# Third aggregation of a graph network: transposed sums, layer products in pairs, later routing, a ring of 14 groups

## What is computed

```python
x = x + gin(layernorm(x), edges)            # two sums over neighbours, four layers
x = x + slice_attention(layernorm(x))
# here the change begins: the sum over neighbours of a GCN layer
h = layernorm(x) @ W
out = segment_sum(h[src] * dinv[src] * dinv[dst], dst) + b
x = x + relu((out - mean) * rsqrt(var + 1e-5) * gamma + beta)
# top-2 of 8 experts, 256 -> 512 -> 256, weights by a softmax of the two gate values
x = x + moe(layernorm(x))
```

## Time and profile before

| what | value |
|---|---|
| median of three timed runs | 4080.15 us |
| the profiled execution, its span | 4526.2 us (the page has no time beside its span) |
| PE, POOL busy | 75%, 62% of the span |
| third aggregation | 2783 to 4060 us: 1277 us |
| its gathers | 846, from 2783.0 to 4009.8 us |
| expert stage | 4060 to 4526 us |

### The profile page before, as it was taken

The page is one execution under the profiler, slowest core; times in us unless marked ns, Lnnn a source line. Parts: engine busy times, 40 slices in busy tenths (PEclk is TensorE's granted clock), DMA queues, the critical chain, the costliest instruction groups (busy, mean ns, idle before and its releaser), DMA issues. The chain is left out here.

```text
span 4526.2 us, 40559 instructions
## 1 busy us (share of the span) xinstructions
PE 3407.3 (75%) x12357; PEld 2256.3 (50%) x12359; DVE 1481.5 (33%) x5707; ACT 497.8 (11%) x1161; POOL 2794.2 (62%) x2815
## 2 busy tenths in 40 slices
PE   3577777878878889899999976566556656658997
PEld 2354444545453444444444455345444444438986
DVE  5112121212121433444333445234343343442221
ACT  4010000000110000000000002000000000003432
POOL 4666666666646666666666502666666666635664
PEclk7788888988889999999999987777777778769998
DMA  6333333433349666666666527334334333327887
GB/s 199 90 112 112 111 110 110 131 111 111 109 128 330 194 198 200 193 190 194 195 201 205 170 104 240 108 114 123 115 117 128 115 114 114 119 80 174 203 210 188
DMA packets 321341, 687.10 MB, mean 152 GB/s; under 512 B 58976, under 2 KB 148300, under 8 KB 320854
## 3 DMA queue, kind: packets, MB, share of 16 engines
q0 software_dynamic: 169712, 474.01, 37.9%
q10 hardware_dynamic: 86448, 110.35, 7.4%
q1 hardware_dynamic: 64970, 100.14, 6.8%
HBM read 592.43 MB, written 99.13 MB: 153 GB/s over the span
## 5 line engine op out<-in xcount | busy, mean ns | idle before, releaser
L280 POOL DMA_INDIRECT s_edge_rows<-table,w_src_idx x2538 | 2495.4, 983 | 1235.3 <-issue 712.6
L320 PE MATMUL s_psA<-s_edge_rows,s_onehot 128*128 128x257 f32 (+2 forms) x4932 | 1695.0, 487 | 212.1 <-DMA s_edge_rows<-table,w_src_idx 92.3
L320 PEld LDWEIGHTS s_psA<-s_edge_rows,s_onehot 128*128 128x128 f32 x4932 | 1012.6, 210 | 758.6 <-issue 635.1
L295 DVE TENSOR_SCALAR s_onehot<-w_iota_row,w_dst_l 128x128 f32<-128x128 bf16 x2466 | 531.6, 296 | 28.5 <-PEq L149 16.4
L2031 POOL DMA_INDIRECT acc_rows<-s_y,s_tnode x105 | 166.3, 1584 | 130.7 <-DVE s_y L2154 98.8
L1011 PE MATMUL s_psM<-s_h1T,s_w1b 128*128 128x512 f32 (+2 forms) x448 | 195.2, 582 | 52.5 <-ACT s_h1T L913 49.0
L330 PE MATMUL s_psA<-s_edge_rows,s_early 128*128 128x257 f32 (+2 forms) x648 | 221.3, 468 | 10.2 <-issue 9.0
L1017 PE MATMUL s_psM<-s_w2a,s_hT 128*128 128x512 f32 x392 | 196.3, 647 | 22.7 <-issue 16.6
L2179 PE MATMUL s_psU<-s_xT,s_w 128*128 128x128 f32 x1680 | 208.2, 278 | 0.2 <-ACT s_xT L2085 0.2
L2179 PEld LDWEIGHTS s_psU<-s_xT,s_w 128*128 128x128 f32 x1680 | 199.3, 195 | 0.6 <-issue 0.6
L2189 PE MATMUL s_psD<-moe_w,s_hT 128*128 x840 | 199.5, 381 | 0.0
(11 more groups left out here) (364 smaller groups left out, 2802.6 us busy)
## 6 DMA issues: line engine op xcount, KB each, us to landing
s_w<-in_L_ffn_W_dram SPq DMA_DIRECT2D x105, 512.0 KB
s_edge_rows<-table,w_src_idx POOLq DMA_INDIRECT x2538
s_swT<-swt_rows SPq DMA_DIRECT2D x12, 1024.0 KB
table<-s_trow ACTq DMA_DIRECT2D x11, 1024.0 KB
own_rows<-s_own ACTq DMA_DIRECT2D x11, 1024.0 KB
s_self_h<-own_rows ACTq DMA_DIRECT2D x11, 1024.0 KB
swt_rows<-s_swT ACTq DMA_DIRECT2D x11, 1024.0 KB
extra_rows<-w_zeros SPq DMA_DIRECT2D x7, 896.0 KB
```

The costliest lines, as they stand in the source:

```text
L280: pool.indirect_dma_start(self.rows[:, g % self.SLOTS, t, :], None, self.table, bass.IndirectOffsetOnAxis(ap=src_idx[:, at:at + 1], axis=0 ...
L295: last = nc.vector.tensor_scalar(into[:, t, :], iota_row[:, q * P:(q + 1) * P], dst_l[:, at + t:at + t + 1], None, ALU.is_equal)
L320: last = nc.tensor.matmul(banks[b % 2][:, 0:w], self.onehot[:, g % self.AHEAD, t, :], self.rows[:, g % self.SLOTS, t, col:col + w], start= ...
```

## The change

It touches the third aggregation alone (`pipeline` gets an argument that the others leave at 0).

- The rows are the weights now and the one-hots the moving operand (`turned_sums`), once for each half of the 256 features. So `psA` holds the sums transposed, and ScalarE copies them straight into `aggT` (`close`). `agg`, the addition on VectorE and the transposes go.
- The own rows are added by PE: two products of `self_v` with the identity matrix, ahead of a block's last group. `self_v` and `extra` have two buffers and are loaded one super-block ahead.
- The ring of gathered groups has 14 slots instead of 6.
- Layer products, scalings and the transposes of `TURNED` go in pairs of blocks, through two whole banks. The scaling (`SCALED`) is a piece of its own, one step behind the product, and so are `TOP` behind `GATES` and `COUNTED` behind `RANK`. The gate products go to `psR`.
- `USED` is at 22 to 25: these four steps run within the next super-block's pieces (`late`), and `at_lane` and `at_tile` have eight buffers instead of four.

```diff
-        def pipeline(group, close, piece, begin=None, close_first=False):
+        def pipeline(group, close, piece, begin=None, close_first=False, late=0):
+            def pieces(s, k):
+                if 0 <= s < len(SUPER):
+                    piece(s, k)
+                if 0 <= s - 1 < len(SUPER) and k < late:
+                    piece(s - 1, STEPS + k)
...
+            def turned_sums(self, pe, b, i, banks, s_free):
...
+                for t in range(n):
+                    for k in range(self.turned):
+                        last = nc.tensor.matmul(banks[b % 2][:, k * P:(k + 1) * P], self.rows[:, g % self.SLOTS, t, k * P:(k + 1) * P],
+                                                self.onehot[:, g % self.AHEAD, t, :],
...
-            PRODUCT, NORM, TURNED, GATES = (0, 1, 2, 3), 4, (7, 8, 9, 10), 11
-            CHOICE, RANK, PLACED, USED = 12, 16, (17, 18, 19, 20), (18, 19, 20, 21)
-            edges = Edges(S, table3, D, ((0, D),), FP32, 1, slots=6)
+            PRODUCT, SCALED, NORM, TURNED, GATES = (1, 3), (2, 4), 5, (9, 10), 12
+            TOP, CHOICE, RANK, COUNTED = 13, 14, 16, 18
+            PLACED, USED = (19, 20, 21, 22), (22, 23, 24, 25)
+            LATE_STEPS = USED[-1] + 1 - STEPS
+            edges = Edges(S, table3, D, ((0, D),), FP32, 1, slots=14, turned=KD)
...
                 def close(b):
                     s, q = place_of(b)
-                    act.wait_ge(s_tr, b + 1)
-                    ac.activation(aggT[:, :, q * P:(q + 1) * P], psT[0][:, 0:D].rearrange("p (k n) -> p k n", k=KD),
-                                  ACT.Copy).then_inc(s_aggT, 1)
+                    if q == 0 and s:
+                        act.wait_ge(s_o, pairs(s)[0][0])
+                    act.wait_ge(edges.s_used, groups_before(b + 1))
+                    ac.activation(aggT[:, :, q * P:(q + 1) * P], psA[b % 2][:, 0:D].rearrange("p (k n) -> p k n", k=KD),
+                                  ACT.Copy).then_inc(s_evac, 1)
...
-                    dve.wait_ge(edges.s_used, groups_before(b + 1))
-                    dve.wait_ge(s_both_self, s + 1)
-                    v.tensor_tensor(agg[:, q, :], self_v[:, q, :], psA[b % 2][:, 0:D], ALU.add).then_inc(s_evac, 1)
...
-                    edges.sums(pe, b, g, psA, s_evac)
+                    if g == groups_of(b) - 1:
+                        s, q = place_of(b)
+                        pe.wait_ge(s_both_self, s + 1)
+                        for k in range(KD):
+                            last = mm(psA[b % 2][:, k * P:(k + 1) * P], self_v[:, s % 2, q, k * P:(k + 1) * P], ident[:, :],
+                                      start=False, stop=False, skip_group_check=True)
+                        last.then_inc(s_own, 1)
+                    edges.turned_sums(pe, b, g, psA, s_evac)
...
-                    pe.wait_ge(s_evac, b + 3)
-                    pe.wait_ge(s_aggT, b + 1)
-                    for k in range(KD):
-                        last = nc.tensor.transpose(psT[0][:, k * P:(k + 1) * P], agg[:, q, k * P:(k + 1) * P], ident[:, :])
-                    last.then_inc(s_tr, 1)
```

More of the change, by code:

```diff
@@ L200, in pipeline @@
                         if s and i == 2 + k * (len(turns) - 2) // STEPS:
-                            piece(s - 1, k)
+                            pieces(s - 1, k)
             close(NB - 1)
             for k in range(STEPS):
-                piece(len(SUPER) - 1, k)
+                pieces(len(SUPER) - 1, k)
+            for k in range(late):
+                pieces(len(SUPER), k)
         def place_of(b):
@@ L1654, in build @@
             s_dve = S.sem("dve_chain")
-            s_self = S.sem("self_rows")
+            s_self = [S.sem(f"self_rows{i}") for i in range(2)]
             s_both_self = S.sem("self_rows_summed")
@@ L1678, in build, with pairs @@
             block = stack.enter_context(nc.Block())
+            def pairs(s):
+                first = sum((nb + 1) // 2 for _, nb in SUPER[:s])
+                return [(first + p, 2 * p, min(2, SUPER[s][1] - 2 * p)) for p in range((SUPER[s][1] + 1) // 2)]
             @block.gpsimd
@@ L1817, in piece @@
                     b0, nb = SUPER[s]
[L1818 to L1819 removed]
+                    if k in SCALED[0:len(pairs(s))]:
+                        at, j, n = pairs(s)[SCALED.index(k)]
                         if j == 0:
@@ L1916, in piece @@
                             pe.wait_ge(s_we, 16)
-                            pe.wait_ge(s_aggT, b0 + nb + 1)
-                        pe.wait_ge(s_acc, b0 + j + 1)
-                        for c in range(KD):
-                            last = mm(psO[(b0 + j) % 2][:, 0:D], aggT[:, c, j * P:(j + 1) * P], w[:, c, :], start=c == 0, stop=c == KD - 1)
-                        last.then_inc(s_o, 1)
-                    if k in TURNED[0:nb]:
-                        j = TURNED.index(k)
-                        if j == 0:
-                            pe.wait_ge(s_gread, s + 1)
-                        pe.wait_ge(s_xl, b0 + j + 5)
-                        pe.wait_ge(s_t1c, b0 + j + 1)
-                        for c in range(KD):
-                            last = nc.tensor.transpose(psT[1][:, c * P:(c + 1) * P], xl3[:, j, c * P:(c + 1) * P], ident[:, :])
+                        pe.wait_ge(s_evac, b0 + j + n + 2)
@@ new lines, in piece @@
+                        pe.wait_ge(s_acc, at + 1)
+                        for i in range(j, j + n):
+                            for c in range(KD):
+                                last = mm(psO[at % 2][:, (i - j) * D:(i - j + 1) * D], aggT[:, c, i * P:(i + 1) * P], w[:, c, :],
+                                          start=c == 0, stop=c == KD - 1)
+                        last.then_inc(s_o, 1)
+                    if k in TURNED[0:len(pairs(s))]:
+                        at, j, n = pairs(s)[TURNED.index(k)]
+                        pe.wait_ge(s_xl, b0 + j + n + 4)
+                        pe.wait_ge(s_t1c, at + 1)
+                        for i in range(n):
+                            for c in range(KD):
+                                last = nc.tensor.transpose(psT[at % 2][:, (2 * c + i) * P:(2 * c + i + 1) * P], xl3[:, j + i, c * P:(c + 1) * P], ident[:, :])
```

117 lines of the change are left out of this document (67 added, 50 removed).

## The result

| kernel | median | range | runs |
|---|---|---|---|
| before | 4080.15 us | 4075.96 to 4080.58 | 5 |
| changed | 4092.51 us | 4090.22 to 4096.16 | 5 |

The ratio is 1.0029, 95% interval 1.0018 to 1.0040: the changed kernel is 12 us slower. The forecast was 4047 us, 33 us faster.

What follows compares the result with a forecast made beforehand. GpSimd's gathers, one per 1.26 us, were taken to pace the third aggregation, with 149.8 us of stops. From 4080.15, 30 (a fifth of the stops) and 3.4 (tail) were subtracted, giving 4047 us, range 3918 to 4100.

Steps and rivals of the forecast that it cites:

- The bound: Third aggregation: GpSimd's 846 gathers, one per 1.26 us, are the pacer, at least 1066 us in the profiled execution.
- The 150 us of stops: Third aggregation: GpSimd stands still 149.8 us beyond its gather rhythm, where the ring of six groups is full.
- the loop PE, VectorE, PE: Third aggregation: ring stops are paid through PE and VectorE waiting in turn; such waits end at L1907, 180.7 us idle.
- From the profile to the clock: Whole kernel: 446 us of the 4526.2 us profile do not exist when timed; 30 of 149.8 us taken as gained.
- the two readings: Where the 446 us lie: first, stops in three aggregations, 449.5 us; second, gathers of 1.00 us when timed, 440 us.
- Own rows: Third aggregation: 98 PE products, 22 us, replace 98 transposes and 49 VectorE additions; the wait at L1907 goes.
- no work is added: Third aggregation, pairs and later routing: same products and copies, fewer handovers, no added work.
- Transposed sums: Third aggregation: shorter, more numerous PE instructions add 16 us of PE work; cost on the path 0, bounds -0 and +16.
- Head and tail: Third aggregation: a 3.3 us head stop, part of the 149.8; at the end 3.96 us shrink to 0.5, saving 3.4.
- No stops when timed: Third aggregation: gathers pace it throughout, so deeper ring and shorter loop give nothing; 4075 us, chance 0.25.
- PE becomes the bound: Third aggregation: at half clock PE needs 1128 us against 1066 for the gathers; 4110 us, chance 0.17.
- All stops are real: Third aggregation: gathers take 1.00 us when timed and the stops exist, so 149.8 us go; 3927 us, chance 0.20.

Runs made afterwards that it cites:

- e0_before: The kernel before, unchanged, profiled again in a session where it takes about 4080 us: 4081.77 us, ratio 0.9995.
- e1_ring6: The changed kernel with the third aggregation's ring back at 6 groups: 4096.66 us, 1.0032 to the kernel before.
- e2_before_ring14: The kernel before with only its third aggregation's ring enlarged to 14 groups: 4084.86 us, ratio 1.0000.
- e10_after_again: The changed kernel, unchanged, in a session where the kernel before takes 4494.65 us: 4514.84 us, ratio 1.0047.
- f2_before_ring14: The kernel before with only the ring of 14 groups, in a session where the kernel before takes 4529.52 us: 4545.80 us, ratio 1.0039.
- g1_no_two_source: The changed kernel with extra rows added on PE and relu and residual taken from PSUM: 4078.64 us, 0.9986 to the kernel before.

## Why the prediction was wrong, point by point

- *The bound.* Right for timed runs: GpSimd's gathers, every 1.26 us, pace the stage, and PE is idle over 350 us. The 150 us of stops, and the loop PE, VectorE, PE behind them, were not there: PE's idle time at L1907 is 180.7 us in the earlier trace rows and 1.8 in the trace of the 4080 session:

```profile
L1907 PE MATMUL s_psT<-w_ident,s_agg 128*128 128x128 f32 x98 | 24.9, 345 | 1.8 <-DVE s_agg L1804 1.8
```

- *From the profile to the clock: the first step that failed.* The 446 us were laid on the profiler. Of the two readings the first was right in what it said of the stops (they belong to that execution: 449.5 us there, 28 in e0_before, so some 422 of the 446), the second (gathers of 1.00 us when timed) wrong. I then stood between the two and took a fifth of 149.8, 30 us, a share that no row gave. The term measured is 0: slots 6 or 14 make no difference (e1_ring6, e2_before_ring14). The 6 us of the Trainium skill, "Runtime: NRT & Kernel Launch" (The launch sequence), were called contradicted by 446 us, but the span and the median were very likely of different kinds of session; in the profiled runs here that have both numbers the span lies 1.8 us under the time, so 6 us above it do not show either.
- *The stops themselves.* The claim "in the profiled execution I take all 149.8 us as gone" is wrong too. In a 4500 session the changed kernel's gathers are idle 392.0 us (e10_after_again), and the ring of 14 alone leaves 397.5 (f2_before_ring14), against 403.6. The 13 us between product and scaling are real in the record, and not a mere matter of VectorE's order: the semaphore event of that product stands at 3323.04, 13.4 us behind the end of its PE rows. Over the stage's 49 products the scaling starts 2.2 us (median, 13.0 at most) behind the product's rows in that trace, 2.5 in f2_before_ring14 and 0.04 in e0_before. Whether PE worked later than its rows say or its signals came late, the trace does not tell.
- *Own rows, and "no work is added": the second step that failed.* I priced the earlier addition by its wait and by the one-hots it stands among, and at nothing for its effect on GpSimd. Its place costs 8.1 us, the normalisation's new moment 3.2, the rest 0.9: 12.2 us in the sum where 0 stood.
- *Transposed sums.* Right in a 4080 session: 42 us more PE, no cost (g1_no_two_source). The bound of +16 was not needed.
- *Head and tail.* No stop of the ring at the head in either kernel (one idle of 1.57 us, the same in both), so nothing to gain. The tail's 3.4 us for certain: the handover from the last placement to the first scaling shrank from 3593.52 - 3589.72 = 3.8 to 3602.30 - 3600.29 = 2.0, but from the last gather to that scaling it is 19.9 us before and 21.2 now, since PE has more in front of it. Term: 0.
- *The rivals.* "No stops when timed" (4075, 0.25) has the right mechanism, and lacks the 12 us of stretched gathers; its tail was not there either. "PE becomes the bound" (4110, 0.17) had 4085 to 4140, and 4092.51 lies in that by luck: PE is idle 358 of 1108.6 us. Nearest to it comes a 4500 session, where the changed kernel loses 1.0047 - 1 of 4495, 21 us. "All stops are real" did not occur. No rival had VectorE slow GpSimd.
- *Signs that came true by luck.* The gathers' idle time was to fall from 403.6 to about 255 us and the third aggregation from 1277 to about 1125. The changed trace has 257.5 and, from its first gather to the expert stage's, 1138. Both come from the session: e0_before, without the change, has 257.5 and 1126. The range 3918 to 4100 holds the result, though its direction, faster with 0.62, is wrong.

Left open: what puts a session into the slow condition; where some 4 of the 6 us by which g1_no_two_source beats the kernel before come from, of which its gathers explain 1.6; what decides for starts within 0.1 us of each other; and why the gathers end no earlier with 14 groups in a 4500 session, so that the longer tail (79 us in e10_after_again, 82 in f2_before_ring14, against 58 with six groups) comes on top, about the 17 to 21 us lost there.

## What to carry to other kernels

Before arguing from a profile, hold its span against the timed runs; at a difference of a tenth, profile again. If GpSimd's indirect DMAs pace a stage, the moment at which VectorE runs a wide instruction with two operands in SBUF can be part of the critical path, though VectorE idles: keep one operand in PSUM, let PE add (g1_no_two_source does both), or see in the trace that it starts 0.1 to 0.2 us behind a gather's start, not before and not much later. A deeper ring took away one short wait here (3.6 us at the head); where the consumer was behind throughout (f2_before_ring14) it only moved the wait to the end.

## What the runs showed that I had not expected

- A gather (0.96 us) beside an instruction on 128x1024 fp32 elements with two operands in SBUF takes up to 2.10 us, by where the two starts lie to each other; beside a reduction of the same length 0.96. With one operand in PSUM (L1867, 0.48 us, 48 times) the gathers it starts in are 0.02 us longer in all.
- Instructions with one tensor and a scalar per partition cost a little too: in the changed kernel some 50 gathers are 0.08 us longer beside one-hots. And the gathers hold up the one-hots: 94 of 598 took 0.41 us on average instead of 0.29.
- With the changed order in a 4500 session, PE starts matmuls 0.7 or 1.4 us apart with its data ready, in stretches, mostly at the half clock. From the first to the last gather of e10_after_again, 1221 us, 634 us are at half clock (1.2 GHz) and hold 227 pauses of 0.25 to 2.6 us (199 us); the changed kernel in a 4080 session has 376 us at half clock and 31 such pauses (48 us) in them.
- In a 4500 session VectorE takes PE's layer products 2.5 us behind their rows (median, f2_before_ring14), in a 4080 session 0.04 us (e0_before).
